# Local attention: the copies of the mixed value tiles on ScalarE in place of GpSimd

## What is computed

```python
def local_attention(q, k, v):                 # 8 heads of 64, windows of 64 tokens
    bq = q.reshape(b, h, w, WINDOW, d) * QK_SCALE
    bk, bv = look_around(k), look_around(v)   # each window with the one before it: 128 keys
    sim = jnp.einsum('bhwid,bhwjd->bhwij', bq, bk)
    mask = (i < j) | (i > j + WINDOW) | (j == -1)
    sim = jnp.where(mask, -jnp.finfo(sim.dtype).max, sim)
    attn = jax.nn.softmax(sim, axis=-1)
    out = jnp.einsum('bhwij,bhwjd->bhwid', attn, bv)

def _layer(x, ...):
    qkv = shift_token(x) @ wqkv               # q, k, v; q and k normed, scaled and rotated
    x = x + local_attention(q, k, v) @ wo
    h = layernorm(shift_token(x)) @ w1 + b1
    a, g = jnp.split(h, 2, axis=-1)
    return x + (a * gelu(g)) @ w2 + b2
```

## Time and profile before

| | us |
|---|---|
| median of 3 runs | 814.53 |
| lowest, highest | 814.22, 815.98 |
| the profiled execution | 814.73 |
| its span in the profile | 812.9 |

### The profile page before, as it was taken

One profiled execution on the slowest core, in us unless ns is written; L12 is line 12 of the kernel. 1 busy time (PEld: TensorE's weight loads), 2 busy tenths in 40 slices (PEclk: granted clock), 3 DMA queues, 4 the chain that ended last, 5 costly groups with the idle time before them and its releaser, 6 DMA issues.

```text
span 812.9 us, 13454 instructions
## 1 busy us (share of the span) xinstructions
PE 643.8 (79%) x4866; PEld 397.2 (49%) x4866; DVE 570.6 (70%) x1187; ACT 500.1 (62%) x1205; POOL 234.2 (29%) x229
## 2 busy tenths in 40 slices
PE   7579985876889989958989787756788697488866
PEld 3222232453456656635555455524576463367555
DVE  7882328547999989577777775499745559984565
ACT  4469978643778868424576576464556449355742
POOL 5030022010988969841000000002633000063500
PEclk8879987878555555565799999886698999659998
DMA  9400000000000000000000000000000000000000
GB/s 300 154 1 1 2 1 0 0 1 0 1 2 2 1 1 1 1 1 0 1 2 1 1 2 1 0 1 1 1 2 2 1 0 1 1 2 2 2 1 26
DMA packets 9062, 10.58 MB, mean 13 GB/s; under 512 B 2747, under 2 KB 7845, under 8 KB 8869
## 3 DMA queue, kind: packets, MB, share of 16 engines
q1 hardware_dynamic: 8996, 9.73, 3.7%
HBM read 9.21 MB, written 0.52 MB: 12 GB/s over the span
## 4 chain that ended last, share of the span: by engine, by line
PE 43%; DVE 33%; ACT 11%; issue 8%; POOL 3%; DMA 1%; ACTq 0%; DVEq 0%; POOLq 0%
PE ps L1401 5%; PE ps L1661 4%; DVE s_nmB L1049 4%; PE ps L1564 4%; PE ps L1644 3%; ACT arena L536 3%; PE ps L1681 2%; PE ps L1472 2%; PE ps L1551 2%; PE ps L1748 2%; PE ps L1756 2%; PE ps L1853 2%; PE ps L1444 2%; PE ps L1389 2%; ACT dev L665 2%
## 5 line engine op out<-in xcount | busy, mean ns | idle before, releaser
L385 POOL TENSOR_SCALAR arena<-arena,s_rB,s_zpu 128x512 uint8<-128x512 f32 x128 | 115.9, 943 | 42.6 <-DVE s_rB L1022 41.3
L574 ACT ACTIVATE arena<-ps,s_nmB 128x512 f32<-128x512 f32 x128 | 86.6, 683 | 31.8 <-DVE s_nmB L1049 31.2
L596 ACT ACTIVATE arena<-ps,s_nmx 128x512 f32<-128x512 f32 (+3 forms) x128 | 60.7, 527 | 49.7 <-DVE s_nmx L1147 49.2
L1049 DVE TENSOR_REDUCE s_nmB<-ps 128x2 f32<-128x1024 f32 x64 | 77.3, 1217 | 6.9 <-PE ps L1551 6.6
L420 POOL COPY arena<-arena 64x512 f32<-64x512 f32 x16 | 12.6, 790 | 240.7 <-PE ps L1748 238.9
L1142 DVE TENSOR_REDUCE s_nmx<-ps 128x1 f32<-128x512 f32 (+3 forms) x128 | 56.6, 483 | 20.5 <-PE ps L1647 20.1
L536 ACT ACTIVATE arena<-ps 128x1024 f32<-128x1024 f32 x64 | 60.9, 1026 | 6.5 <-PE ps L1456 6.5
L1564 PE MATMUL ps<-cst,arena 128*128 128x128 f32 x256 | 61.9, 422 | 1.2 <-ACT arena L566 0.8
L1407 PE MATMUL ps<-ones 128*128 128x512 f16 x134 | 44.1, 493 | 22.7 <-ACT s_wn L507 6.6
L1564 PEld LDWEIGHTS ps<-cst,arena 128*128 128x128 f32 x256 | 49.3, 221 | 14.4 <-POOL arena L385 7.9
L1551 PE MATMUL ps<-staged 8*128 8x512 f16 x128 | 46.6, 585 | 11.8 <-ACT arena L574 10.9
(11 more groups left out here) (346 smaller groups left out, 1567.0 us busy)
## 6 DMA issues: line engine op xcount, KB each, us to landing
vec<-in_vec SPq DMA_DIRECT2D x1, 1882.0 KB, 11.9
w_d<-in_wqkv SPq DMA_DIRECT2D x2, 768.0 KB
vec<-in_vec SPq DMA_DIRECT2D x1, 960.0 KB, 8.1
w_h<-in_w SPq DMA_DIRECT2D x2, 341.0 KB
x_tok<-in_x SPq DMA_DIRECT2D x1, 512.0 KB, 4.1
arena<-in_w_f SPq DMA_DIRECT2D x2, 256.0 KB, 7.8
rope<-in_rope SPq DMA_DIRECT2D x1, 512.0 KB, 10.5
w_do<-in_wo SPq DMA_DIRECT2D x2, 256.0 KB
```

The costliest lines, as they stand in the source:

```text
L385: nc.gpsimd.tensor_scalar(u8[:, n % 4, j // 2, :, 2 * (j % 2)], prob[:, n % 2, j * 512:j * 512 + 512], sm("rB", 8)[:, c:c + 1], sm("zpu", ...
L574: nc.scalar.activation(prob[:, n % 2, j * 512:j * 512 + 512], ps[:, j, :], ACT.Exp, bias=sm("nmB", 8)[:, c:c + 1], accum_out=sm("sumB", 8) ...
L596: nc.scalar.activation(probC[:, n % 2, at(qt):at(qt) + w], ps[:, bank, col:col + w], ACT.Exp, bias=nmx[:, TB * b + qt, h:h + 1]).then_inc( ...
L1049: free(V.tensor_reduce(sm("nmB", 8)[:, c:c + 2], ps[:, 2 * half:2 * half + 2, :], X, ALU.max, negate=True), "maxB")
```

## The change

The function `mixed_values` moves from GpSimd's program to ScalarE's. GpSimd no longer waits for anything in its loop but the rates. On ScalarE the call stands in even turns behind the four exponentials of the unit and ahead of the squares and of the L675 copy. The copies become activations with the function Copy, of the same 64x512 regions, and count up the same semaphore, `mixD`, without a wait of the issuing engine for its own instruction. The wait for `normD` is gone, the one for `qkT_D` stays.

```diff
             def mixed_values(l, t):
-                b = t // TB
-                pool.wait_ge(sem["qkT_D"], 8 * (B * l + b) + 4)
-                if T * l + t:
-                    pool.wait_ge(sem["normD"], 2 * (T * l + t))
-                step(nc.gpsimd.tensor_copy(qkvD[0:WINDOW, t, 0:INNER], qkvD[0:WINDOW, t, 2 * INNER:3 * INNER]), "mixD")
-                if t % TB:
-                    step(nc.gpsimd.tensor_copy(qkvD[WINDOW:P, t, 0:INNER], qkvD[WINDOW:P, t - 1, 2 * INNER:3 * INNER]), "mixD")
...
-                        if u % 2 == 0:
-                            mixed_values(l, TB * b + u // 2)
                         pool.wait_ge(sem["ratesD"], U + 1)
...
+                def mixed_values(l, t):
+                    act.wait_ge(sem["qkT_D"], 8 * (B * l + t // TB) + 4)
+                    nc.scalar.activation(qkvD[0:WINDOW, t, 0:INNER], qkvD[0:WINDOW, t, 2 * INNER:3 * INNER], ACT.Copy)\
+                        .then_inc(sem["mixD"], 1)
+                    if t % TB:
+                        nc.scalar.activation(qkvD[WINDOW:P, t, 0:INNER], qkvD[WINDOW:P, t - 1, 2 * INNER:3 * INNER], ACT.Copy)\
+                            .then_inc(sem["mixD"], 1)
...
                                                      accum_out=sm("sumD", 16)[:, c:c + 1]).then_inc(sem["expD"], 1)
+                        if u % 2 == 0 and u < TB * 2:
+                            mixed_values(l, TB * b + u // 2)
                         if b == 1 and u == 6:
                             squares_d(0)
```

More of the change, by code:

```diff
@@ L412, in _ @@
             again_c(pool, 1, nc.gpsimd.tensor_copy)
-            def mixed_values(l, t):
-                b = t // TB
-                pool.wait_ge(sem["qkT_D"], 8 * (B * l + b) + 4)
-                if T * l + t:
-                    pool.wait_ge(sem["normD"], 2 * (T * l + t))
-                step(nc.gpsimd.tensor_copy(qkvD[0:WINDOW, t, 0:INNER], qkvD[0:WINDOW, t, 2 * INNER:3 * INNER]), "mixD")
-                if t % TB:
-                    step(nc.gpsimd.tensor_copy(qkvD[WINDOW:P, t, 0:INNER], qkvD[WINDOW:P, t - 1, 2 * INNER:3 * INNER]), "mixD")
             for l in range(DEPTH):
```

## The result

| | median of the runs | span of the profiled execution | mean granted clock |
|---|---|---|---|
| before | 814.99 us (814.22 to 815.98, 4 runs) | 812.9 us | 0.784 |
| with the change | 826.87 us (825.89 to 828.42, 4 runs) | 826.6 us | 0.772 |

The ratio is 1.0147, with a 95% interval of 1.0125 to 1.0169: the change makes the kernel 1.5% slower, 11.9 us. The direction was forecast, the size was not: 818.5 us, and 821.2 as the end of the range. The copies cost somewhat more than the sum said, 4 to 5 us. What they did to TensorE's clock is the larger part, 7 to 8 us net of what the clock had cost the kernel before.

The account below looks back on a forecast made before the run. No engine is full; a chain of waits bounds the kernel, in batch 1 ScalarE's queue. Per layer 2.3 us lost in batch 1 less 0.4 gained in batch 0, 3.8 for two layers on 814.73: 818.5 us, range 815.4 to 821.2.

Parts of the forecast that it names:

- What bounds the kernel: Local attention: a chain through several engines, none full; VectorE and GpSimd obstruct each other in batch 0, ScalarE's queue in batch 1.
- Batch 0, 0.4 us gained per layer: Batch 0: 0.5 us gained without GpSimd's copies, less 0.1 for turn 6's pair on ScalarE.
- The wait of 0.40: Batch 0: TensorE's transposes wait 0.40 us for unit 2's multiplication, held behind GpSimd's copies; this goes.
- the tail of 0.2: Batch 0: a VectorE rotary instruction stretched 0.20 us (0.89 against 0.69) by a GpSimd copy's tail; this goes.
- the 1.41: Batch 0: a VectorE rotary instruction of 1.41 us against 0.69, stretched by unit 4's multiplication; this stays.
- The price of a copy: Each ScalarE copy holds the queue 0.58 us, bounds 0.48 and 0.60; a pair 1.16 us.
- Where the pairs land: Batch 1: pairs of turns 2 and 6 cost 1.16 us each, 2.3 per layer; turns 0 and 4 are free.
- Rival 1: Batch 1, TensorE's clock: falls in layer 2 too, 821.2 us, chance 0.13; or stays high in layer 1, 815.8, 0.09.
- The base: The forecast was added to the profiled execution's own 814.73 us, called fair beside the runs' median of 814.53.
- Rival 2: Batch 1 takes the pairs in, the delay of turns 2 and 6 made up later: 813.9 us, chance 0.12.
- Rival 3: Batch 0: both stretched VectorE rotary instructions run at 0.69 us, and batch 1 hides its pairs: 812.1 us, chance 0.08.
- The likeliest case: The forecast itself: 1.9 us more per layer, 3.8 for two layers, 818.5 us, chance 0.58.

Follow-up runs that it names:

- The fill of the kernel before: Kernel before, with six dummy TensorE matmuls ahead of the L675 wait in turns 3 and 7 of batch 1: 810.75 us (0.9983).
- the filled kernel: Changed kernel, with six dummy TensorE matmuls ahead of the L675 wait in turns 3 and 7 of batch 1: 816.14 us (1.0035).

## Why the prediction was right or wrong

- **What bounds the kernel**: right. Batch 0 goes by GpSimd and VectorE, batch 1 by ScalarE's queue, shown by the kernels with the copies of one batch.
- **Batch 0, 0.4 us gained per layer**: right, 0.39 and 0.38. The wait of 0.40 is gone, the tail of 0.2 too, and the 1.41 stays.
- **The price of a copy**: too low. 0.58 was taken from a copy out of PSUM, with 0.60 as the upper end on the ground that copies overlap; the real one, from SBUF, starts the next only 0.65 us later. A pair is 1.30, outside both bounds. It is worth 0.6 us over the four pairs that count.
- **Where the pairs land**: right in place and, at an equal clock, near in size. Turns 2 and 6 count. From unit 3 on they cost between 2.24 and 2.95 us per layer, 2.65 by my estimate, for 2.3 forecast; the difference to the estimate is the price of a copy.
- **Rival 1, the clock**: this is the step that failed, three times over. Its chance: "clock falls in layer 2 too 0.13", while it fell in both layers of each of the three kernels with a pair ahead of L675 in turn 2, at full width and without a fill. The prediction itself said that more idle time speaks for this fall. Its price: one more fall of 2.7 us; measured are 4.7 us per layer against the same kernel with its clock held up. Its reach: it was counted for turn 2 only, but in the changed kernel the wait of turn 7 brings a second fall that goes into the output projection (3.84 to 5.46 us), 1.6 us per layer of stretches that the prediction held to be untouched. With the copies of batch 1 alone the second fall stopped short of it. The stretches behind batch 1 took 2.33 and 3.01 us more in all; beyond the projection that is argued only. And the range ended at this rival's bare value, 821.2, without the bounds of the other terms on top.
- **The account of batch 1**: the pairs 2.4, the clock 4.65, less what the kernel before lost to the clock itself, 39.71 - 37.48 = 2.2, is the +4.83 of layer 1. In layer 2 it is 2.7 + 4.78 - 0.85 = 6.62. These sums close by the way they are made. The fill of the kernel before holds it up by some 0.4 us, which belongs on top of the pairs' share and of the 2.2 and 0.85 alike.
- **The base**: the kernel before was taken as a fixed 814.73. It is a kernel whose clock falls early in batch 1 of layer 1 and late in that of layer 2, with runs from 806 to 817 in the later series. The prediction saw the first in the earlier trace rows and named the 2.7 us, but read it as an accident of layer 1 and not as a sign that both layers stand at the edge: behind a wait of 0.51 the clock sometimes stayed up, and behind one of 1.81 in turn 3 it never did.
- **Rival 2**, taken in: no, 0.28 us of room against 1.30. **Rival 3**, the ports: the 1.41 us instruction was still there, and room before unit 3's exponentials was what decided.

The likeliest case, 3.8 us more, looks near for the filled kernel, which lies 2.8 us above its base. That is in part luck: its clock stays up where that of the kernel before falls. Against the kernel before with the same fill it is 5.4 us.

## What to carry to other kernels

Where TensorE waits in a chain of short steps, price an added wait twice: its own length, and all the TensorE work behind it at 1.2 GHz, on to where the rows show the clock back at 2.4. If the trace of before already shows one of two equal stages at the lower level, count on the other too: behind waits of 1.81 us both fell here, in three kernels. An engine that is 62% busy can take work only where its row shows idle time and no hand-over stands behind; there the same 28 copies cost nothing. Matmuls of no use in the waits that can't be avoided can bring back the clock (from 11.9 to 2.8 us above the kernel before, and in batch 0 from 30.58 to 28.60 us per layer); in a wait that is too short for them they hold up the work, here by 0.7 us.

## What was not expected of the hardware

- These copies on ScalarE, 64x512 from SBUF to SBUF, don't overlap with what follows. All 28 are alike, here with minimum, median and maximum in ns:

```profile
L621 ACT ACTIVATE arena<-arena x16: 624/626/634, 558.2 to 774.9; 64x512 f32<-64x512 f32 x16
L624 ACT ACTIVATE arena<-arena x12: 626/626/627, 565.8 to 775.5; 64x512 f32<-64x512 f32 x12
```

  They start 0.65 us apart; those of 256 columns last 0.41 and start 0.44 apart. Between the exponentials' steps the starts are closer than the durations (0.46 long and 0.44 to the next, with a 0.20 us read between them). The squares behind the pair of turn 6, 128x512 from SBUF to SBUF, last 0.63 us and the next instruction starts 0.54 later. So some forms overlap and this one doesn't; why is open. The Trainium skill, page "ScalarE: Activation LUTs", section "What ACT_TABLE_LOAD costs", gives 186 ns plus 0.833 ns per column, 613 for 512, which agrees with 626; of its overlap of about 93 ns between instructions the pairs show nothing, while the squares agree with it.
- Behind each product of batch 1 that waited 1.7 to 2.1 us unfilled, the clock fell, for one stretch or for several. Behind 1.39 us it fell for one stretch in layer 1 and not in layer 2. Behind 0.5 us it fell in some layers (layer 1 of the kernel before and of the one with no copies) and not in others. The wait alone doesn't decide it, and no run here shows what does. The Trainium skill, page "TensorE: Matmul & The Clock Gate", section "HAM oscillation — how this bites in real kernels", tells of a matmul kernel whose clock goes back and forth between the levels because it waits for DMA between groups of matmuls. Here the waits are for ScalarE, and the trace shows the same back and forth, with 0.89, 0.50, 0.50, 0.83, 1.00, 0.52 in stretches of 4 us.
- Six matmuls of 1.47 us in all, whose result nobody reads, in each of the two long waits of a layer are worth 9.1 us to the changed kernel (11.9 less 2.8, each above its own base); those of turn 3 alone are worth some 8 (11.9 less 3.5).
